# First layer of a two-layer graph network: seven block products gathered in one running bank, and the residual kept in place

## The reference, cut to what matters

```python
# layer 0
mi = einsum('bkd,od->bko', x, W[:, :512])
mj = einsum('bkd,od->bko', x, W[:, 512:])
a = adj.astype(float32); deg = a.sum(axis=1)
x = layernorm(x + deg[:, None] * (mi + b) + einsum('ij,bjo->bio', a, mj))
# layer 1: multi-head attention, 8 heads, masked by adj
q, k, v = heads(x @ Wq.T + bq), heads(x @ Wk.T + bk), heads(x @ Wv.T + bv)
attn = softmax(where(adj == 0, -inf, q @ k.T / 8))
x = layernorm(x + (attn @ v).merged() @ Wo.T + bo)
```

## Time and profile before

| what | value |
|---|---|
| median of 3 runs | 3020.41 us (3019.78 to 3020.76) |
| profiled execution, its own time | 3019.9 us |
| its span, first to last instruction | 3018.1 us |
| granted PE clock, mean | 0.993 |
| PE busy | 98% of the span |
| DVE, ACT, POOL busy | 77%, 57%, 54% |
| DMA | 36 GB/s over the span |

### The profile page before, as it was taken

The page is one execution under the profiler, slowest core; times in us unless marked ns, Lnnn a source line. Parts: engine busy times, 40 slices in busy tenths (PEclk is TensorE's granted clock), DMA queues, the critical chain, the costliest instruction groups (busy, mean ns, idle before and its releaser), DMA issues.

```text
span 3018.1 us, 60894 instructions
## 1 busy us (share of the span) xinstructions
PE 2972.1 (98%) x20096; PEld 2615.4 (87%) x20096; DVE 2317.9 (77%) x5915; ACT 1732.0 (57%) x4622; POOL 1625.5 (54%) x1538
## 2 busy tenths in 40 slices
PE   7999999999999999999999999999999999999997
PEld 5888888888888888888888888888888888888886
DVE  7777777777777777777777777777777777777776
ACT  4556555555565555555655655555556556555554
POOL 4545556555555555565554555555555545556552
PEclk8999999999999999999999999999999999999998
DMA  3010110010101101101001011011010010110100
GB/s 133 22 43 29 35 42 28 35 35 31 38 28 35 42 28 35 42 28 35 35 28 42 28 35 42 28 35 42 28 35 31 31 42 28 35 42 28 35 29 22
DMA packets 49556, 108.48 MB, mean 36 GB/s; under 512 B 3696, under 2 KB 6256, under 8 KB 49520
## 3 DMA queue, kind: packets, MB, share of 16 engines
q1 hardware_dynamic: 49520, 108.02, 10.3%
HBM read 74.46 MB, written 33.55 MB: 36 GB/s over the span
## 4 chain that ended last, share of the span: by engine, by line
PE 98%; DVE 1%; DMA 0%; issue 0%; ACT 0%; POOL 0%; SPq 0%; POOLq 0%; DVEq 0%
PE proj L430 52%; PE proj L472 21%; PE av L430 8%; PE attn L590 7%; PE attn L578 7%; PE proj L526 2%; DMA w_raw<-in_w0T 0%; DMA out<-hb 0%; DVE pT_lo L942 0%; DVE mj_mi L995 0%; DVE mj_lo L942 0%; DVE wji_lo L1104 0%; DVE mj_mi L1001 0%; POOL hb L344 0%; DVE probs L919 0%
## 5 line engine op out<-in xcount | busy, mean ns | idle before, releaser
L735 ACT ACTIVATE probs<-probs,exp_bias 128x256 f32<-128x256 f32 x1024 | 507.8, 498 | 38.8 <-DVE exp_bias L927 37.4
L751 ACT CAST pT_hi<-attn 128x512 fp32r<-128x512 f32 x508 | 272.8, 590 | 377.9 <-PE av L430 318.9
L330 POOL TENSOR_TENSOR probs<-probs,row_inv 128x512 f32<-128x512 f32 x256 | 264.1, 1042 | 393.1 <-DVE row_inv L937 393.1
L942 DVE TENSOR_TENSOR pT_lo<-attn,pT_hi 128x512 fp32r<-128x512 f32 x508 | 326.3, 684 | 85.7 <-ACT pT_hi L751 83.7
L919 DVE CUSTOM_DVE_ANT_0 probs<-attn,mask_add 128x256 f32<-128x256 f32 x1024 | 376.2, 419 | 5.0 <-PE attn L578 2.0
L472 PE MATMUL proj<-wji_hi,xs_hi 128*128 128x512 f32 x896 | 362.0, 404 | 12.7 <-DVE wji_lo L1104 12.7
L472 PE MATMUL proj<-wji_lo,xs_hi 128*128 128x512 f32 x896 | 354.7, 396 | 0.0
L472 PE MATMUL proj<-wji_hi,xs_lo 128*128 128x512 f32 x896 | 354.6, 396 | 0.0
L952 DVE SCALAR_TENSOR_TENSOR oT<-av,bv_cols,o_part 64x256 f32<-64x256 f32 x512 | 243.4, 475 | 121.5 <-POOL oT_lo L358 60.8
L759 ACT COPY o_part<-av 64x512 f32<-64x512 f32 x256 | 149.4, 583 | 318.8 <-PE av L430 317.3
L358 POOL TENSOR_TENSOR oT_lo<-oT,oT_hi 128x256 fp32r<-128x256 f32 x256 | 201.2, 786 | 203.6 <-ACT oT_hi L766 203.6
(11 more groups left out here) (123 smaller groups left out, 8628.7 us busy)
## 6 DMA issues: line engine op xcount, KB each, us to landing
xs_raw<-in_xT SPq DMA_DIRECT2D x64, 512.0 KB, 3.3
xb<-in_x SPq DMA_DIRECT2D x64, 512.0 KB, 3.4
out<-hb SPq DMA_DIRECT2D x64, 512.0 KB, 2.8
w_raw<-in_w0T SPq DMA_DIRECT2D x8, 256.0 KB, 6.0
stage<-in_wqT SPq DMA_DIRECT2D x1, 1024.0 KB, 8.9
stage<-in_wkT SPq DMA_DIRECT2D x1, 1024.0 KB, 11.0
stage<-in_wvT SPq DMA_DIRECT2D x1, 1024.0 KB, 5.3
stage<-in_woT SPq DMA_DIRECT2D x1, 1024.0 KB, 6.5
```

The lines of the kernel that those rows point to most:

```text
L330: pool.tensor_tensor(probs[:, g % 2, 1, :, :], probs[:, g % 2, 1, :, :], row_inv[:, g % 2, R:2 * R].unsqueeze(2).to_broadcast([P, R, N]), ...
L735: last = nc.scalar.activation(e, e, ACT.Exp, bias=exp_bias[:, g % 2, s:s + 1], scale=SCALE, accum_out=row_sum[:, g % 2, s:s + 1])
L751: nc.scalar.copy(pT_tail[g % 2 if tail else 0][0][:, i, :, :], attn[2 * (g % 2) + i][:, :].rearrange("p (k q) -> p k q", k=R)).then_inc(pt ...
L942: V.tensor_tensor(low_[:, i, :, :], attn[2 * (g % 2) + i][:, :].rearrange("p (k q) -> p k q", k=R), high[:, i, :, :].bitcast(F32), ALU.sub ...
```

## The change: what it does

1. **Banks.** The seven products go to U, Z and M (`PRODUCTS`). Four of them (U1 to U4) accumulate on one another in bank U without being restarted: after each one the bank holds another partial sum, which must be read before the next product may start. Z takes two, M one. The order is U1, Z1, U2, M2, U3, Z2, U4.
2. **Reading.** For each product ACT copies the left half of U1, Z1 and U2 to `mj_raw` (`mj_copy`, 128 by 256), and DVE (`l0_sum`) adds the left half of M2, U3 and Z2 to it. The right half, multiplied by the degree, is added by DVE straight onto `xb`, one 128 by 256 instruction for each of the seven products. `l0_x`, `mj_mi`, `first_copy`, `first_sum` and `mi_add` are gone. U4 is not put into `mj_raw`: ACT and DVE make its high and low part from the bank.
3. **xb becomes h.** `xb` is kept twice (`[P, 2, R, D]`), by parity of the sample; the aggregate is added to it, it is normalised in place, transposed, and used as the residual.
4. **Low parts of mj.** POOL makes those of row block 1's right half and of row block 0 (`mj_low`), DVE that of U4's quarter.
5. **SP.** The load of x waits for `hT` and `hb_ready` of the sample two before, not for `mi_added`. At the start x of sample 0 is loaded ahead of the fourth W block and of the weights of layer 1.
6. **Start.** DVE sets 48 single columns of `oT` to zero first (`PADDING`); the degree and degree times bias are computed ahead of the third W block; `W_ORDER` follows the products.

```diff
+PADDING = 48
-    L0_X, L0_Y, L0_Z = 0, 1, 2
-    PRODUCTS = ((1, 0, L0_X), (5, 4, L0_Y), (4, 3, L0_Z), (6, 5, L0_Y), (2, 1, L0_X), (3, 6, L0_Y), (7, 2, L0_Z))
+    L0_U, L0_Z, L0_M = 0, 1, 2
+    PRODUCTS = ((1, 0, L0_U), (4, 3, L0_Z), (5, 4, L0_U), (2, 1, L0_M), (6, 5, L0_U), (7, 2, L0_Z), (3, 6, L0_U))
+    U1, Z1, U2, M2, U3, Z2, U4 = range(7)
-    W_ORDER = (0, 3, 4, 5, 1, 6, 2)
+    W_ORDER = (0, 3, 4, 1, 5, 2, 6)
...
-                    sp.wait_ge(mi_added, R * (b + 2))
-                    load_x(b + 2)
+
+                    sp.wait_ge(done["hT"], 2 * (b + 1))
+                    sp.wait_ge(hb_ready, b + 1)
+                    load_x(b + 2, parity)
...
+            def mj_low(n, part):
+
+                at = mj_raw[:, 1, HD:D], mj_hi[:, 1, HD:D], mj_lo[:, 1, HD:D]
+                if part == 1:
+                    at = mj_raw[:, 0, :], mj_hi[:, 0, :], mj_lo[:, 0, :]
+                raw, high, low_ = at
+                pool.wait_ge(mj_hi_done, 3 * n + (1 if part == 0 else 3))
+                pool.tensor_tensor(low_, raw, high.bitcast(F32), ALU.subtract).then_inc(mj_split, 1)
...
+                elif i in (Z1, M2):
...
                 else:
-                    pe.wait_ge(l0_summed, 5 * n + 2)
-                start = i in (0, 1, 2)
+
+                    pe.wait_ge(l0_read, NP * n + {U2: U1, U3: U2, Z2: Z1, U4: U3}[i] + 1)
+                start = i in (U1, M2, Z1)
...
-
-                pe.wait_ge(mj_row1_split, n + 1)
-                pe.wait_ge(l0_summed, 5 * n + 5)
+                pe.wait_ge(mj_split, 2 * n + 1)
+                pe.wait_ge(l0_read, NP * n + U4 + 1)
...
-                        pe.wait_ge(mj_row0_split, n + 1)
+                        pe.wait_ge(mj_split, 2 * n + 2)
...
+            def mj_copy(n, i):
+                bank_ = proj[PRODUCTS[i][2]][:, 0:HD]
+                row, cols = {U1: (0, slice(0, HD)), U2: (0, slice(HD, D)), Z1: (1, slice(HD, D))}[i]
+                act.wait_ge(l0_done, NP * n + i + 1)
+                nc.scalar.copy(mj_raw[:, row, cols], bank_).then_inc(mj_copied, 1)
+
+            def mj_high(n, part):
+
+                if part == 0:
+                    act.wait_ge(l0_read, NP * n + U3 + 1)
+                    dst, src = mj_hi[:, 1, HD:D], mj_raw[:, 1, HD:D]
+                elif part == 2:
+                    act.wait_ge(l0_read, NP * n + Z2 + 1)
+                    dst, src = mj_hi[:, 0, :], mj_raw[:, 0, :]
                 else:
...
+                    act.wait_ge(l0_done, NP * n + U4 + 1)
+                    dst, src = mj_hi[:, 1, 0:HD], proj[L0_U][:, 0:HD]
+                nc.scalar.copy(dst, src).then_inc(mj_hi_done, 1)
...
+                if i in (U1, U2, Z1):
+
+                    dve.wait_ge(mj_copied, 3 * n + {U1: 1, Z1: 2, U2: 3}[i])
+                elif i == U4:
+                    dve.wait_ge(mj_hi_done, 3 * n + 2)
+                    V.tensor_tensor(mj_lo[:, row, cols], bank_[:, 0:HD], mj_hi[:, row, cols].bitcast(F32), ALU.subtract)
                 else:
...
+                    dve.wait_ge(mj_copied, 3 * n + {M2: 1, U3: 2, Z2: 3}[i])
+                    V.tensor_tensor(mj_, bank_[:, 0:HD], mj_, ALU.add)
+                if i == U1:
+                    dve.wait_ge(xb_ready, n + 1)
+                elif i in (M2, U3, Z2):
+                    dve.wait_ge(l0_read, NP * n + {M2: U1, U3: Z1, Z2: U2}[i] + 1)
+                V.scalar_tensor_tensor(out=h_, in0=bank_[:, HD:D], scalar=deg[:, row:row + 1], in1=h_,
+                                       op0=ALU.mult, op1=ALU.add).then_inc(l0_read, 1)
...
+            for j in range(PADDING):
+                V.memset(oT[:, j:j + 1], 0.0)
```

More of the change, by code:

```diff
@@ L263, in _, with load_block @@
             load_xT(0)
-            for i, (kh, oh) in enumerate(W_LOADS):
+            def load_block(i):
+                kh, oh = W_LOADS[i]
                 for kind in range(2):
@@ L269, in _ @@
                                      block_loaded[i], 16)
+            for i in range(3):
+                load_block(i)
             sp.dma_start(adjT_i.rearrange("p (r n) -> p r n", r=R),
@@ L381, in _ @@
                 x_low(1, part)
-            add_bias(1)
+            add_bias(1, 1)
             pool.wait_ge(bias_loaded, 64)
@@ L406, in step @@
                     x_low(b + 2, 1)
-                if ahead: add_bias(b + 2)
+                if ahead: add_bias(b + 2, parity)
                 split_o(b, 2)
@@ L514, in last_y, with transpose_h @@
                             last.then_inc(done["y"], 1)
-            def transpose_h(n, half, first=False):
+            def transpose_h(n, half, parity, first=False):
                 if half == 0:
@@ L639, in _ @@
                 first_layer(0, i, first=True)
-            pe.wait_ge(adj_ready, 1)
+            pe.wait_ge(adj_ready, 2)
             aggregate(0)
             for half in range(2):
-                transpose_h(0, half, first=True)
+                transpose_h(0, half, 0, first=True)
             for half in range(2):
```

226 lines of the change are left out of this document (86 added, 140 removed).

## The result

The changed kernel takes 3015.64 us (median of 20 runs, 3014.35 to 3017.05), the kernel before 3020.73 us in the same comparison (20 runs, 3019.54 to 3022.99). The ratio is 0.9983, with a 95% interval of 0.9976 to 0.9990. The prediction was 3015.3 us. In the comparison of e1 to e4 three executions took far longer (6183.45 us of the kernel before, 11069.62 and 10274.4 us of e3), no trace shows why, and the ratios and the median of e3 leave them out. The profiled execution took 3016.6 us, with a span of 3014.8 us; before it was 3018.1 us.

The account below looks back on a forecast made before the run. The prediction took PE to bound the kernel (98%), with one loop weight load late behind DVE. Loop -6.0, first step -0.75 and start +1.6 gave -5.15 us, so 3015.3 us for the median; range 3010 to 3026.

Parts of the forecast that it names:

- the rule "loss = lateness - 0.17": PE weight loads in the loop: a load can be 0.17 us late before PE loses time.
- U2 waits for the read of U1: Each loop step: DVE's read of U1 makes U2's load 0.19 to 0.28 us late; loss taken as 0.03 us.
- U3, U4 and the first half: Each loop step, loads of U3, U4 and the aggregate's first half: nothing lost at any.
- Second half of the aggregate: Each loop step: POOL's low part makes the load 0.12 to 0.24 us late; loss taken as 0.01 us.
- Sum of a step: Loop: 0.137 gained less 0.03 and 0.01, 0.096 us per step; times 62 steps, -6.0 us.
- The reason for the gain: Aggregate's second half in the loop: a mi_add ahead on DVE made L986 late; its removal gains 0.137 us per step.
- First step, -0.75: First step's aggregate end: DVE adds row block 0 at about 75.8 instead of 76.54, -0.75 us.
- The start, +1.6: Kernel start: DVE and POOL block each other; aggregate's second half at about 32.8 against 30.82, sum +1.6 us.
- Memsets at nothing: DVE's start: the 48 memsets end at 4.6, just after DVE's first wait; price 0 to 0.6 us, taken as 0.
- the first (U1's read late in each step): Loop: register work delays U1's read, its load is 0.55 us late, PE loses 0.38 per step; 3037 us, chance 0.15.
- The second (nothing lost at U2): Loop: no loss at U2 nor at the aggregate, the read as short as a 0.42 sum; 3012.7 us, chance 0.15.
- The third (the start takes it back): Start: memsets +0.6 and a late fourth W block +2 leave about 1.5 of the gain; 3018.8 us, chance 0.18.

Follow-up runs that it names:

- e1: Kernel before with one DVE pair swapped per step, the low part of row block 0 ahead of the first mi_add: 3013.43 us, ratio 0.9976.
- e4: Changed kernel with the start's bias add onto x of sample 0 on DVE instead of POOL: 3016.44 us, ratio 0.9987 to the kernel before.
- e3: Changed kernel without its 48 memsets: 3116.1 us, median of four executions, ratio 1.0325.
- e5: Changed kernel with the read of U1 one place later on DVE, behind the next two row maxima: 3059.11 us, ratio 1.0130.
- e2: Changed kernel with the read of U1 on DVE moved ahead of the maximum before it: 3012.37 us, ratio 0.9974 to the kernel before.
- e9: Changed kernel with both U1 read earlier on DVE and the start's bias add on DVE instead of POOL: 3010.99 us, ratio 0.9970 to the kernel before.
- e10: Kernel before with the same 48 memsets put at DVE's start: 3021.08 us, ratio 1.0002.
- e6: Changed kernel with the 48 memsets moved behind the loop, to the end of DVE's program: 3116.0 us in one run.
- e7: Changed kernel with 24 memsets instead of 48 at DVE's start: 3017.46 us in one run.
- e8: Changed kernel with 96 memsets instead of 48 at DVE's start: 3017.24 us in one run.

## Why the prediction was right

The total was right (3015.3 against 3015.64), and the largest term held in mechanism, with 4.4 of the 6.0 us foretold. That the total is so close is in part luck: in the profiled execution the loop gave 1.6 us less than forecast, the first step 1.1 more, and the start took 1.5 more, which makes -3.3 in place of -5.15. The medians lie nearer (-5.1), but executions of the changed kernel lie up to 2.7 us apart.

1. *What bounds, and the rule "loss = lateness - 0.17".* Right. The rule was read from one place of before and held at another load, from 0.24 to 0.93 us of lateness (table under e5).
2. *U2 waits for the read of U1.* Right in mechanism, with the value chosen near the optimistic bound. The read starts at T+2.31 and takes 478 ns on average, and the load was worked out to be 0.19 to 0.28 us late: it is 0.236. By the prediction's own rule that is 0.07 lost per step. The prediction took 0.03, from a start at the early end; the runs show 0.06 to 0.08.
3. *U3, U4 and the first half cost nothing.* Right: the loads show one waited-for instruction, and without it (e2) the step is within 0.02 us of e1's.
4. *Second half of the aggregate.* Right that nothing is lost. POOL's low part was worked out to end at 1554.09 to 1554.21 for T = 1541.71, that is T+12.38 to T+12.50. It ended at 1552.16 + 1.29 = 1553.45, T+12.39. The predicted wait of 0.1 to 0.2 us on POOL does not appear in the view of waits, but the load begins at 1553.50, 0.05 behind POOL's end, so POOL did set it. The pairs of matmuls still follow one another at 0.48 and 0.46 us, about two spacings of 0.233.
5. *Sum of a step.* Predicted -0.096, with 62 steps -6.0. Measured 46.18 - 46.11 = -0.073 over 61 steps, -4.4. The reason is point 2, and 0.7 us in one step, the first of the loop: it takes 46.74 (203.50 to 250.24 in the chain), and its load for U2 is the one that waits 0.9. Ahead of the read of U1, DVE's bias of the exponentials took 1.16 us there, where the next step has 0.56. Why it did, no run shows:

```profile
204.63 1.16 DVE L935 TENSOR_SCALAR exp_bias<-row_max 128x4 f32<-128x4 f32 x1
```

6. *The reason for the gain.* The prediction says that the `mi_add` ahead of L986 made it late. e1 shows this alone: it removes the wait and gives 46.03.
7. *First step, -0.75.* Measured -0.87 up to the norm's end, and so in other executions: 18.37 to 18.41 us in after, e2, e3, e4 and e9, 19.24 and 19.25 in before and e10. The clock behind the norm, which the prediction left out, gave another 1.0 us in this execution (0.68 against 0.56). With e2, 5.3 us for that stretch, and with e9, which has the same steps, 6.2, this is not a property of the change.
8. *The start, +1.6.* The blocking was right, the working was short of two waits, and the total comes near what most runs show. U1 was to be read near 20.0 and was read at 20.25, though the first block was late by 0.65; so the blocking of POOL and DVE was sized well, and e4 shows it (3.37 to 1.22). But the second half of the aggregate came at 34.30, where 32.8 was worked out, 1.5 later. Of this 0.25 is there at the read of U1. The rest is that the prediction ran DVE's work end to end and left out two of its waits: 0.90 for ACT's copy of U2, whose six matmuls still lie 0.43 us apart behind PE's idle 3.95, and 0.41 for PE once more (0.25 + 1.31 = 1.56). The faster matmuls of the aggregate gave 0.8, not 0.4: DVE adds it at 35.20 against 32.53, 2.67 later, where the second half is 3.48 later. In this execution the products of the loop's first step start 3.14 later than before. It is the latest of its kind: with the same work at the start they begin between 63.0 and 64.7 in e2, e3, e5, e6, e7 and e8, against 61.8 to 62.4 in before, e1 and e10. The middle of these seven, 63.5, is 1.2 behind before's 62.28, near the predicted 1.6. With it in place of 65.42 the pieces of the result add up to -5.2, as the medians do (-5.1).
9. *Memsets at nothing.* Right for their time (0.029 each, over at 2.2, and e10), and blind to what they are for. Taking them only as a cost, the prediction had no rival in which they prevent a loss.

Of the rivals, the first (U1's read late in each step) did not happen: no gap lies between the READ and the read. Its 0.18 us of register work was itself too large by its own rows: with the 0.51 us that the prediction uses elsewhere for a product to be seen, in place of 0.43, 0.10 is left. But e5 shows that the rule that priced it holds: 0.7 us later in the order makes the kernel 1.3% slower than before. The second (nothing lost at U2) did not happen either, since the read takes 478 ns and not 420; e2, which takes the loss away, comes to the time that this rival gave (3012.37 against 3012.7). The third (the start takes it back) is what the profiled execution half shows, with +3.14 in the start, and the medians do not.

Measured against the Trainium skill: "SBUF — State Buffer", section "SBUF: two separate sides", says that DVE and GpSimd hold a shared port pair exclusively, also against a DVE instruction with two SBUF inputs. This case's trace agrees, with 3.37 beside POOL and 1.22 without it, and with POOL's 3.19 behind DVE's low part. Its page "VectorE: DVE Perf Modes", the section on the TRN2 errata, gives an estimate of 392 ns for the new instruction (120 + 256 cycles at 0.96 GHz); the trace has 478 ns over 413 of them, and the measurement decides.

## What to carry to other kernels

Where PE is the bound, read in the waits of its weight loads which single buffer comes late, how late, and what stands ahead of the writer or reader on its engine; swapping two neighbours there can be worth as much as a new way of gathering. Turn the lateness into time by what the loads can be late for nothing (here 0.17 us) and check it by moving the same instruction one place each way. If an edit changes the number or the order of instructions in a loop, look for a pause of type "issue" at the head of each turn and at the packets of the instruction queue before judging the edit itself. Some dozens of short instructions ahead of the loop can move it to a better place.

## What the runs showed of the hardware

- A loop can wait for its own instructions. With 0, 128 or 256 memsets ahead of the loop DVE's loop touches four blocks of 128 instructions and the instruction queue has 156 to 158 packets; with 24, 48 or 96 it touches three and there are 16 or 17. In e3 DVE pauses for about 2.5 us per turn of two steps, and each branch back of the bad kernels brings five packets. The bad places cost about 100 us here, and repeat every 128 instructions.
- A memset of one column in 128 partitions takes 0.029 us on DVE, well below the smallest instruction in the rows of before (0.08).
- Two SBUF additions of 1024 columns, one on POOL and one on DVE, take 3.19 and 3.37 us together, where the DVE one takes 1.22 alone.
- At the start PE's matmuls of 512 columns lie 0.43 us apart from the first one at 10.39 up to 25.7 us (512 columns in 0.43 us is the pace of 1.2 GHz), with idle stretches of 0.67 and 3.95 us among them, and then 0.233, while the granted clock is shown as 1.00 in that stretch. In before, which worked without such a gap from 15.62 on, the change comes at 18.8.
- The stretch behind the first step's norm takes 5.3 to 6.4 us for the same 42 matmuls (41 in e9's record), at a mean granted clock of 0.71 to 0.54. e2 and e9 have the same steps and lie 0.9 us apart in it, so this spread is one between executions. In the last step the same 24 matmuls take 5.87 us at a granted clock of 1.00 or 7.40 at 0.77.
